# Two graph layers on one core: plain fp32 projections instead of split products, and softmax sums made on TensorE

## What is computed

```
q, k, v = x @ Wq + bq, x @ Wk + bk, x @ Wv + bv        # 6 heads of 64
p = softmax(q k^T / 8 + bias(adj));  x1 = layernorm(x + (p v) @ Wf + bf)

h = x1 @ W                                             # 12 heads of 32
th = tanh(h);  s[a,n,m] = th[a,n] . w_src[a] + th[a,m] . w_dst[a]
s = leaky_relu(s, 0.2), masked by adj;  p1 = softmax(s)
f = elu(p1 h + b);  gate = sigmoid(x1 @ H_w^T + H_b)
out = layernorm(x1 + gate * f + (1 - gate) * x1)
```

## Time and profile before

| | |
|---|---|
| median of 3 runs | 1132.66 us (1132.14 to 1134.66) |
| the profiled execution | 1132.1 us |
| its span, first to last instruction | 1130.2 us |
| TensorE, matmuls (PE) | 1073.2 us busy, 95% of the span, 8236 records |
| TensorE, weight loads (PEld) | 883.3 us, 78% |
| VectorE (DVE) | 897.2 us, 79% |
| ScalarE (ACT) | 919.4 us, 81% |
| GpSimd (POOL) | 765.2 us, 68% |
| mean granted clock of TensorE | 0.986 of 2.4 GHz |

### The profile page before, as it was taken

The page is one execution under the profiler, slowest core; times in us unless marked ns, Lnnn a source line. Parts: engine busy times, 40 slices in busy tenths (PEclk is TensorE's granted clock), DMA queues, the critical chain, the costliest instruction groups (busy, mean ns, idle before and its releaser), DMA issues.

```text
span 1130.2 us, 25501 instructions
## 1 busy us (share of the span) xinstructions
PE 1073.2 (95%) x8236; PEld 883.3 (78%) x8236; DVE 897.2 (79%) x1828; ACT 919.4 (81%) x3383; POOL 765.2 (68%) x909
## 2 busy tenths in 40 slices
PE   6889999999999999999999999999999999997774
PEld 5678888888888888878888888888888888786652
DVE  5457878888887888888788888878888887888874
ACT  3348888888888888888888888888888888888874
POOL 1367776676777667677766767776676777667652
PEclk9999999999999999999999999999999999999986
DMA  9101010020101002010100201010020101000000
GB/s 270 56 2 57 15 68 18 8 71 16 64 15 61 26 8 71 16 64 15 62 26 8 71 15 64 15 60 27 8 72 16 64 15 43 16 8 16 16 15 21
DMA packets 25893, 44.66 MB, mean 40 GB/s; under 512 B 2462, under 2 KB 23714, under 8 KB 25762
## 3 DMA queue, kind: packets, MB, share of 16 engines
q1 hardware_dynamic: 23234, 41.91, 10.9%
q10 hardware_dynamic: 2496, 1.12, 0.5%
q0 software_dynamic: 32, 0.00, 0.0%
HBM read 30.43 MB, written 12.58 MB: 38 GB/s over the span
## 4 chain that ended last, share of the span: by engine, by line
PE 57%; POOL 23%; issue 9%; DVE 6%; ACT 3%; DMA 2%; POOLq 0%; ACTq 0%; DVEq 0%
PE ps_b L253 13%; PE ps_d L253 13%; POOL z L964 9%; PE ps_a L253 7%; PE ps_d L459 5%; POOL xT_lo L916 4%; PE ps_a L382 3%; PE ps_s L362 3%; PE ps_s L354 3%; PE ps_d L447 3%; POOL p L991 3%; PE ps_c L469 2%; POOL s L956 2%; POOL thw L999 2%; POOL y L958 2%
## 5 line engine op out<-in xcount | busy, mean ns | idle before, releaser
L583 ACT ACTIVATE z<-z,s 128x128 f32<-128x128 f32 x768 | 297.1, 391 | 1.5 <-DVE s L798 0.9
L964 POOL TENSOR_TENSOR z<-z,mask 128x512 f32<-128x512 f32 x192 | 218.2, 1164 | 0.5 <-ACT z L679 0.5
L583 ACT ACTIVATION_READ_ACCUMULATOR z<-z,s 128x1 f32 x768 | 146.6, 191 | 0.0
L610 ACT ACTIVATE p<-ps_s,s 128x128 f32<-128x128 f32 x384 | 134.7, 378 | 13.1 <-DVE s L776 13.0
L991 POOL TENSOR_TENSOR p<-p,s 128x768 f32<-128x768 f32 x64 | 94.2, 1471 | 61.4 <-DVE s L804 61.4
L459 PE MATMUL ps_d<-ident,z 128*128 128x128 f32 x768 | 118.7, 278 | 9.2 <-ACT z L583 8.2
L953 POOL TENSOR_SCALAR s<-s 128x1 f32<-128x1 f32 x128 | 28.8, 225 | 143.3 <-DVE s L895 131.6
L999 POOL TENSOR_TENSOR thw<-th,w_sd 128x768 f32<-128x768 f32 x64 | 117.4, 1834 | 3.7 <-ACT th L633 3.7
L459 PEld LDWEIGHTS ps_d<-ident,z 128*128 128x128 f32 x768 | 90.6, 143 | 17.6 <-ACT z L583 9.1
L679 ACT ACTIVATE z<-ps_d 128x512 f32<-128x512 f32 x192 | 100.8, 598 | 1.2 <-PE ps_d L447 1.2
L945 POOL TENSOR_TENSOR xb<-xb,bf_all 128x768 f32<-128x768 f32 x32 | 58.6, 1834 | 58.6 <-DVE sd L878 55.5
(11 more groups left out here) (154 smaller groups left out, 3448.5 us busy)
## 6 DMA issues: line engine op xcount, KB each, us to landing
x_cols<-in_xT_dram SPq DMA_DIRECT2D x16, 768.0 KB, 6.4
xb<-in_x_dram SPq DMA_DIRECT2D x16, 768.0 KB, 4.9
out_dram<-y SPq DMA_DIRECT2D x64, 192.0 KB, 1.8
z<-in_L_gnn_Wq_dram SPq DMA_DIRECT2D x1, 576.0 KB, 6.4
p1T<-in_L_gnn_Wk_dram SPq DMA_DIRECT2D x1, 576.0 KB, 8.7
qT<-in_L_gnn_Wv_dram SPq DMA_DIRECT2D x1, 576.0 KB, 11.1
kT<-in_L_gnn_Wf_dram SPq DMA_DIRECT2D x1, 576.0 KB, 13.4
z<-in_L_gnn_W_dram SPq DMA_DIRECT2D x1, 576.0 KB, 11.7
```

Of the source, the lines that this page charges most:

```text
L583: done = act.activation(z[:, a, :], z[:, a, :], ACT.Exp, bias=neg1[:, a:a + 1], accum_out=sum1[:, a:a + 1])
L610: last = act.activation(p0[:, o, i, :], ps_s[:, o, i * N:(i + 1) * N], ACT.Exp, bias=neg0[:, k:k + 1], accum_out=sum0[:, k:k + 1])
L964: pool.tensor_tensor(z[:, 4 * q:4 * q + 4, :], z[:, 4 * q:4 * q + 4, :], mask[:, t, :].unsqueeze(1).broadcast_to([P, 4, N]), ALU.add).then ...
```

## The change

Weights and activations are held once, in fp32 (`weights`, xT with two halves by the group's parity, x1T, ctxT), and loaded straight into place. `product` makes one matmul a chunk. All hi copies and lo subtractions go. The x load of the next group waits for the v products of the group before the present one's (`v_made`).

ScalarE's twelve exps of the second layer no longer accumulate. A constant sum_pick (128 rows; three blocks of 32 columns, in block q column q is all ones) is made at the start on GpSimd. Behind `apply_p1`'s product twelve more matmuls multiply p1T by it into ps_c[:, 384:512], so that partition 32k + q holds the sums of head 4q + k. The copy to fT takes all 512 columns, `turn_f` turns four blocks, the sums' first, and VectorE's reciprocal reads the sums from ps_c and waits for `f_turned`; `turn_sd` waits for that reciprocal, since it writes to the same columns.

```diff
-            def split_product(out_ap, lhs, rhs, chunks=range(C), closed=True):
+            def product(out_ap, lhs, rhs, chunks=range(C), closed=True):
 
                 for c in chunks:
-                    for k, (a, b) in enumerate(HI_LO):
-                        last = pe.matmul(out_ap, lhs(a, c), rhs(b, c), start=(c == 0 and k == 0),
-                                         stop=(closed and c == C - 1 and k == 2))
+                    last = pe.matmul(out_ap, lhs(c), rhs(c), start=(c == 0), stop=(closed and c == C - 1))
                 return last
...
                 for c in range(C):
-                    for k in range(2):
-                        last = pe.matmul(ps_s[:, 0, 0:D], bv_col[:, c:c + 1].broadcast_to([P, P]),
-                                         w_parts["wf"][k][:, c, :].bitcast(F32), start=(c == 0 and k == 0),
-                                         stop=(c == C - 1 and k == 1))
+                    last = pe.matmul(ps_s[:, 0, 0:D], bv_col[:, c:c + 1].broadcast_to([P, P]),
+                                     weights["wf"][:, c, :], start=(c == 0), stop=(c == C - 1))
...
             def turn_sd(t):
 
                 pe.wait_ge(S["sd3_ready"], t + 1)
+                if due(t - 1):
+                    pe.wait_ge(S["inv1_ready"], t - 1)
...
                         last = pe.matmul(ps_c[D1 * (a % 4):D1 * (a % 4 + 1), q * N:(q + 1) * N],
                                          h[:, par2, a, :], p1T[:, a, :], start=True, stop=True)
+
+                if t == 0:
+                    pe.wait_ge(S["sum_pick_ready"], 1)
+                for q in range(3):
+                    for k in range(4):
+                        last = pe.matmul(ps_c[D1 * k:D1 * (k + 1), D:D + N], sum_pick[:, D1 * q:D1 * (q + 1)],
+                                         p1T[:, 4 * q + k, :], start=(q == 0), stop=(q == 2))
                 last.then_inc(S["ph_made"], 1)
...
-                for c in range(C):
+                for c in (C, 0, 1, 2):
                     last = pe.transpose(ps_c[:, c * P:(c + 1) * P], fT[:, c, :], ident[:])
...
-                        done = act.activation(z[:, a, :], z[:, a, :], ACT.Exp, bias=neg1[:, a:a + 1],
-                                              accum_out=sum1[:, a:a + 1])
+                        done = act.activation(z[:, a, :], z[:, a, :], ACT.Exp, bias=neg1[:, a:a + 1])
...
-                        act.activation(fT[:], ps_c[:, 0:D].rearrange("p (c n) -> p c n", c=C),
+                        act.activation(fT[:], ps_c[:].rearrange("p (c n) -> p c n", c=C + 1),
                                        ACT.Copy).then_inc(S["fT_ready"], 1)
...
-                    if gat:
-                        lo_part(x1T, ps_b, slice(0, N), "x1_hi", tl + 1, "x1_lo")
                     if has_tail(n, j, 2):
 
                         t2 = tl - 2
-                        dve.wait_ge(S["exp1_ready"], 3 * (t2 + 1))
-                        dve.reciprocal(inv1, sum1).then_inc(S["inv1_ready"], 1)
+                        dve.wait_ge(S["f_turned"], t2 + 1)
+                        dve.reciprocal(inv1.rearrange("p (q k) -> p q k", q=3),
+                                       ps_sums.rearrange("p (k q) -> p q k", k=4)[:, 0:3, :]
+                                       ).then_inc(S["inv1_ready"], 1)
                         dve.wait_ge(S["inv1_ready"], t2 + 1)
-                        dve.wait_ge(S["f_turned"], t2 + 1)
...
-                    if att:
-                        dve.wait_ge(S["ctx_made"], ta + 1)
-                        lo_part(ctxT, ps_a, slice(0, N), "ctx_hi", ta + 1, "ctx_lo")
...
-                    if qkv and n + 1 < NG and j == 3:
-                        x_lo(g + 1, 0)
-                        x_lo(g + 1, 1)
```

More of the change, by code:

```diff
@@ L77, in build_program @@
         minus_one = sb("minus_one", [P, 1])
[L79 to L80 removed]
+        weights = {n: sb(n, [P, C, D]) for n in ("wq", "wk", "wv", "wf", "w1", "hw")}
         bq_col = sb("bq_col", [P, C])
@@ L89, in build_program @@
         mask = sb("mask", [P, B, N], BF16)
-        x_cols = sb("x_cols", [P, C, G * N])
-        xT = [sb("xT_hi", [P, C, G * N], F32R), sb("xT_lo", [P, C, G * N], F32R)]
+        xT = sb("xT", [P, 2, C, G * N])
         xb = sb("xb", [P, 2, G, D])
@@ L100, in build_program @@
         p0T = sb("p0T", [P, 2, C, N])
-        ctxT = [sb("ctxT_hi", [P, C, N], F32R), sb("ctxT_lo", [P, C, N], F32R)]
+        ctxT = sb("ctxT", [P, C, N])
         r0 = sb("r0", [P, D])
@@ L106, in build_program @@
         x1 = sb("x1", [P, 2, G, D])
-        x1T = [sb("x1T_hi", [P, C, N], F32R), sb("x1T_lo", [P, C, N], F32R)]
+        x1T = sb("x1T", [P, C, N])
         h = sb("h", [P, 2, H1, D1])
@@ L122, in build_program @@
         s2 = sb("s2", [P, 64])
-        inv1, sum1 = s2[:, 0:12], s2[:, 40:52]
+        inv1 = s2[:, 0:12]
         st1, mv1, ve1, rs1, nm1 = s2[:, 16:22], s2[:, 24:26], s2[:, 28:29], s2[:, 30:31], s2[:, 32:33]
-        fT = sb("fT", [P, C, N])
+        fT = sb("fT", [P, C + 1, N])
+        sum_pick = sb("sum_pick", [P, 3 * D1])
+        ps_sums = ps_c[:, D:D + N]
         ps_f = ps_c[:, 0:D].rearrange("p (a e) -> p a e", a=H1)
@@ L394, in project_out @@
                         pe.wait_ge(S["r0_ready"], t)
-                    pe.wait_ge(S["ctx_lo"], t + 1)
+                    pe.wait_ge(S["ctx_ready"], t + 1)
                     if n == 1 and j == 0:
-                        pe.wait_ge(S["weight_lo"], 4)
-                last = split_product(ps_b[:, 0:D], lambda a, c: ctxT[a][:, c, :],
-                                     lambda b, c: w_parts["wf"][b][:, c, :], chunks)
+                        pe.wait_ge(S["weight_in_3"], 16)
+                last = product(ps_b[:, 0:D], lambda c: ctxT[:, c, :], lambda c: weights["wf"][:, c, :], chunks)
                 if chunks[-1] == C - 1:
@@ L542, in _ @@
             act.activation(bq8[:], bq_col[:], ACT.Copy, scale=D0 ** -0.5).then_inc(S["bias_ready"], 1)
-            def x_hi(g, half):
-                at = slice(2 * half * N, 2 * (half + 1) * N)
-                act.wait_ge(S["x_in_ready"], 16 * (g + 1))
-                if due(G * (g - 1) + 2 * (half + 1)):
-                    act.wait_ge(S["v_made"], G * (g - 1) + 2 * (half + 1))
-                act.activation(xT[0][:, :, at], x_cols[:, :, at], ACT.Copy).then_inc(S["x_hi"], 1)
-            x_hi(0, 0)
-            x_hi(0, 1)
-            for n in range(3):
-                act.wait_ge(S[f"weight_in_{n}"], 16)
-                act.activation(w_parts[W_ORDER[n]][0][:], stage[n], ACT.Copy).then_inc(S["weight_hi"], 1)
             act.wait_ge(S["bias_ready"], 1)
@@ L637, in iteration @@
                         evacuate_v(2)
-                    if qkv and n + 1 < NG and j == 3:
-                        x_hi(g + 1, 1)
                     if att:
@@ L853, in iteration @@
                         evacuate_v(3)
-                    if n == 0 and j < 3:
-                        weight_parts(3 + j)
                     if n == 0 and j == 3:
@@ L922, in _ @@
             pool.memset(hb_rows[:], 0.0).then_inc(S["padding_ready"], 1)
+            pool.memset(sum_pick[:], 0.0).then_inc(S["sum_zeroed"], 1)
+            pool.wait_ge(S["sum_zeroed"], 1)
+            pool.memset(sum_pick[:, 0:2 * D1 + 3:D1 + 1], 1.0).then_inc(S["sum_pick_ready"], 1)
             pool.memset(minus_one[:], -1.0).then_inc(S["minus_one_ready"], 1)
```

126 lines of the change are left out of this document (43 added, 83 removed).

## The result

The changed kernel takes 1286.76 us (1285.82 to 1287.65, four runs); the kernel before took 1132.40 beside it (1132.07 to 1134.66). The ratio is 1.1358, interval 1.1338 to 1.1378: slower, by 154.4 us. The forecast was 1292.5, range 1266 to 1330. The profiled execution has a span of 1284.0 us against 1130.2.

A forecast was written before the change was run, and what follows sets the result against it. TensorE's streaming was taken as the bound: +195.9 us of streaming less 35.5 us coming back on the 1130.2 us span gave 1290.6, forecast as 1292.5 us, range 1266 to 1330.

The forecast's parts named there:

- 384 and 512 columns: Projection products in plain fp32: +0.36 us each at 384 columns, +92.2 in all; +0.50 each at 512, +48.0 in all.
- the bias product: Product over Wf, already plain fp32 at 0.323 us a record; it loses half its records, -1.9 us.
- The sums: Softmax sums on TensorE: twelve small plain fp32 products a graph, 0.79 us, +50.6 us over 64 graphs.
- What comes back: Stalls and idle time expected to shrink, at logits, first graphs of groups, start and last graphs; -35.5 us in all.
- The logits: Three 512-column records a graph, 0.93 us where 0.69 would do; 0.15 us back by 60 graphs, -9 us.
- the longer first graph of a group: 0.35 us extra behind GpSimd's two xT_lo subtractions, expected to go: -5 us over 15 groups.
- Up to 86 us: Early graphs, TensorE busy 42 of 48 us from 38 on; -4 us taken of the 6 idle.
- The start: Launch start: TensorE waits for the load alone, -3 us, and a shorter bf_all wait, -1.5; -4.5 taken.
- the wait for bf_all: TensorE's 2.04 us wait before the first mask, expected shorter without VectorE's six weight parts ahead: -1.5 us.
- The last graphs: Last six graphs, four without projections: about -1 us net in place of the +11.9 counted, so -13 us.
- That the sums overlap: Sum records in different column quarters overlap; the rival, one after another, 2.59 us a block, 1408 us, had chance 4%.
- The faster rival: Projection products: plain records as quick as fp32r ones, two a chunk for three, graph set by 15.0 us loop; 1043 us, chance 3%.

The follow-up runs named there:

- plain_only: Changed kernel with plain fp32 products kept but the softmax sums given back to ScalarE's accumulating reads; 1243.69 us, ratio 1.0979 to the kernel before.
- sums_only: Kernel before with split products kept and only the softmax sums moved to TensorE; 1171.68 us, ratio 1.0341.
- two_r_records: Kernel before with two fp32r records a chunk instead of three, one low-part product left out, low parts still made; 1100.05 us, ratio 0.9719.
- high_only_sums: Kernel before with only high-by-high products, low parts neither made nor used, and softmax sums on TensorE; 1091.61 us, ratio 0.9647.
- one_r_record: Kernel before with one fp32r record a chunk, only high by high, low parts still made; 1129.21 us, ratio 0.9961.
- quarter_by_quarter: Changed kernel with the two loops of the sum product swapped, so three matmuls in a row use the same column quarter; 1332.40 us, ratio 1.1763.
- reads_back: Changed kernel with ScalarE's accumulating reads put back beside TensorE's sums, their results unused; 1289.41 us, ratio 1.1385.

## Why the prediction was right

The mechanism and the large terms held: TensorE's stream was the bound, a plain record costs 0.323 us over 384 columns and 0.43 over 512, and the freed time of the others was worth little. That the total came within 6 us is in part luck, since the misses have both signs: the sums and small pieces of a graph were priced too high, the start and the last graphs too low. By its own steps:

- *384 and 512 columns.* 1.94 and 2.58 us a product, exactly as worked out; the 512-column record, for which before had no row, goes with the columns (2.58/6 = 0.430). With the bias product they are +138 us of the sum; plain_only measured +110.7 in total, less what came back.
- *The sums.* Taken at 0.79 us from the product ahead, measured 0.66: -8 us over 64 graphs, the largest single miss. The trace says why. The two products run alike, six waves of four records 109 ns apart, 0.65 us. The 0.79 holds one thing more, the step to the scores that follow: their first record starts 0.22 us after the last wave and not 0.11. That step is paid once, whether or not the sums stand ahead of it; in the changed kernel the product with h, now followed by the sums, takes 0.68 us from start to start. So a row was read as the price of a product where it held the change to the next kind as well. The estimate by the Trainium skill's page "TensorE: Matmul & The Clock Gate", section Back-to-back issue gap, 81 ns for each, would be 1.94 us; the trace doesn't agree, with 0.77 us from start to start in this order and 1.49 in the other, and the measurement decides.
- *What comes back.* The logits gave 0.11 (0.93 to 0.82) for 0.15, and the longer first graph of a group vanished, as said. A graph came to 18.53 us for a forecast 18.8; half of the difference is the sums. Up to 86 us -4 was taken; TensorE's idle time between 38 and 86 us fell from 6.1 to 3.7.
- *The start.* TensorE begins at 7.53 us instead of 11.12, a little better than the 3 us forecast. But its first records run at half pace, and the wait for bf_all did not shrink:

```profile
7.53 5.46 PE L240 MATMUL ps_a<-xT,wq 128*128 128x512 f32 x6 [7.53 <-DMA wq<-in_L_gnn_Wq_dram]
12.78 2.91 PE L240 MATMUL ps_b<-xT,wq 128*128 128x512 f32 x6
...
38.29 0.48 PE L325 MATMUL ps_s<-mask,ident_b 128*128 128x384 bf16 x2 [2.63 <-DVE bf_all L802]
```

  Six records in 5.25 us are 0.875 each, twice 0.43, the lower clock. The kernel before had that too, for 2.7 us: its first seven records start between 11.12 and 13.82, 0.45 apart for 0.23 later. So of the 3.6 us of the earlier start the slow records take 1.3 back. And the small constants on VectorE stand behind the copy of the fourth v block in its order; with TensorE later, they are later. The first mask is at 38.29, 0.75 later than in the earlier trace rows, where the terms had it 2 us earlier.
- *The last graphs.* Taken at -1 us net. The graphs without projections are 16.11 us apart for 15.0:

```profile
1180.57 0.88 PE L363 MATMUL ps_a<-p0T,v 128*64 128x128 f32 x12
...
1196.67 0.88 PE L363 MATMUL ps_a<-p0T,v 128*64 128x128 f32 x12
```

  That is +4.4 for four, where I had counted 2.4 (five chunks). What I left out is the sums: TensorE makes the scores behind them, ScalarE's exps of p come later, and GpSimd waits 0.89 us before it scales p where it waited 0.34. The two halves agree: without projections plain_only's last graphs are 15.53 us apart with a wait of 0.32, sums_only's 15.77 with one of 1.12. From the last of these starts to the end it is 1284.0 - 1228.88 = 55.1 for 1130.2 - 1072.55 = 57.7. Net +1.9 instead of -1.
- *The rivals.* That the sums overlap was confirmed, and that their time hangs on their order. The faster rival's condition didn't occur, and no run has its price, two quick records a chunk with no low parts to make. The nearest speak against 1043: two_r_records, which still makes them, takes 1100, and high_only_sums, with one record and no low parts, 1092. Its loop of 15.0 us was taken from graphs without projections, while in two_r_records the graphs with v and the first of a group take 16.35 and 16.7. The point from which it would decide, 0.237 us a record, was never near 0.323.

## What to carry to other kernels

Price a matmul change in array time, not in instructions: count records, columns and the distance between their starts, and look in the trace for one small instance of the new kind, as the bias product was here; and see what follows the row that you take a price from, since the step to another kind of matmul may be in it. Work taken off engines with free time does nothing while another engine's stream is full, and work moved onto that engine costs nearly its full length; the way to see it is a table by stages and a chain that stays on one engine. And where TensorE starts to wait inside a loop, look at the granted clock of its pieces there before forecasting a gain from removing its work: in one_r_record it was at half in two graphs of three.

## What the runs showed of the hardware that I had not expected

- With one fp32r record a chunk instead of two, 15% of all of TensorE's records less (7116 to 6060), the kernel was 29 us slower (1100.05 to 1129.21 us). After a wait of 2.4 us its granted clock stood at 0.50 for 4.26 us that lie on the loop; how much of the 29 us that makes is open.
- Small plain fp32 records of 32 stationary and 128 moving columns: four in four column quarters start 7 ns apart and the next four 109 ns later (after). Issued quarter by quarter each row keeps its 109 ns, and the next row begins 0.22 to 0.25 us behind the last, so that 24 records take 1.49 us for 0.77 (quarter_by_quarter).
- From such records to the scores' (64 rows, 128 columns) the first start comes 0.22 us after the last wave, twice the distance of the waves (before and after).
- The accumulating read behind an exp of 128x128 has a record of 191 ns and makes ScalarE 0.08 us busier (after and reads_back).
- At the start of the changed kernel the records run at half pace, 0.875 us for 0.43, for 5.25 us, while the granted clock of the profile reads 1.00 there; at the start of the launch the distance between records told the clock here, and that figure did not.
